# Value products of two head groups set beside the score products in TensorE's order, in an attention block on one core

## What is computed

```
x = _ln(src) * (1.0 + scale) + shift
q = (x @ Wq + bq).reshape(B, S, N_HEAD, HEAD_DIM).transpose(0, 2, 1, 3)
k = ...
v = ...
scores = jnp.einsum('bhqd,bhkd->bhqk', q / math.sqrt(HEAD_DIM), k)
scores = scores + attention_bias
scores = jnp.where(src_mask, -jnp.inf, scores.astype(jnp.float32))
probs = jax.nn.softmax(scores, axis=-1).astype(v.dtype)
ctx = jnp.einsum('bhqk,bhkd->bhqd', probs, v)
ctx = ctx.transpose(0, 2, 1, 3).reshape(B, S, D)
x = x + (ctx @ Wo + bo)
```

## Time and profile before

| | us |
|---|---|
| median of 3 runs | 1367.18 (1366.38 to 1367.87) |
| the profiled execution's own time | 1369.96 |
| its span, first to last instruction | 1367.8 |
| PE busy | 1321.2 (97%) |
| DVE busy | 1075.3 (79%) |
| ACT busy | 1071.8 (78%) |
| POOL busy | 871.5 (64%) |

### The profile page before, as it was taken

One profiled execution on the slowest core, in us unless ns is written; L12 is line 12 of the kernel. 1 busy time (PEld: TensorE's weight loads), 2 busy tenths in 40 slices (PEclk: granted clock), 3 DMA queues, 4 the chain that ended last, 5 costly groups with the idle time before them and its releaser, 6 DMA issues. The chain is left out here.

```text
span 1367.8 us, 39618 instructions
## 1 busy us (share of the span) xinstructions
PE 1321.2 (97%) x11936; PEld 1119.3 (82%) x11936; DVE 1075.3 (79%) x3638; ACT 1071.8 (78%) x2664; POOL 871.5 (64%) x874
## 2 busy tenths in 40 slices
PE   4999999999999999999999998789999999999997
PEld 3777777777777777777777776579999999999997
DVE  4777777787877777778778777578888888888885
ACT  1788888888888888888888886777777777777773
POOL 4999989989999998998999998311222222122210
PEclk9999999999999999999999999989999999999998
DMA  9546656555564665655556482101010110111100
GB/s 289 184 152 200 191 161 207 166 188 181 169 210 152 197 191 159 208 164 187 181 169 210 154 259 70 32 24 40 31 46 31 35 42 31 46 31 41 36 24 32
DMA packets 182670, 175.07 MB, mean 128 GB/s; under 512 B 15552, under 2 KB 182112, under 8 KB 182624
## 3 DMA queue, kind: packets, MB, share of 16 engines
q1 hardware_dynamic: 181248, 173.64, 40.1%
q10 hardware_dynamic: 1376, 0.85, 0.2%
HBM read 157.69 MB, written 16.78 MB: 128 GB/s over the span
## 5 line engine op out<-in xcount | busy, mean ns | idle before, releaser
L428 POOL TENSOR_TENSOR ring<-ring,maskv 128x1024 f32<-128x1024 f32 x256 | 600.0, 2373 | 12.4 <-DMA ring<-in_fside 5.1
L912 ACT ACTIVATE ring<-ring,nmax 128x256 f32<-128x256 f32 x1024 | 452.5, 501 | 24.6 <-DVE nmax L606 24.6
L606 DVE CUSTOM_DVE_ANT_0 ring<-bank,ring 128x256 f32<-128x256 f32 x1024 | 373.0, 418 | 90.4 <-PE bank L1176 73.5
L917 ACT ACTIVATE pT<-bank 128x512 f32<-128x512 f32 x416 | 239.5, 592 | 103.5 <-PE bank L1191 103.4
L1191 PE MATMUL bank<-ident,ring 128*128 128x128 f32 x2048 | 292.6, 278 | 1.4 <-ACT pT L917 1.1
L1191 PEld LDWEIGHTS bank<-ident,ring 128*128 128x128 f32 x2048 | 231.9, 143 | 70.6 <-issue 47.9
L1047 ACT ACTIVATE work<-bank,b1t 128x256 f32<-128x256 f32 x256 | 107.6, 476 | 109.0 <-PE bank L1390 109.0
L1176 PE MATMUL bank<-work 32*128 32x256 f32 x2048 | 148.4, 404 | 6.0 <-DVE nmax L606 5.2
L1390 PE MATMUL bank<-hT_high,w_high 128*128 128x256 f32 x512 | 147.9, 289 | 3.4 <-DVE hT_rest L781 3.4
L1403 PE MATMUL bank<-w_high,gT_high 128*128 128x256 f32 x512 | 148.1, 289 | 0.0
L1403 PE MATMUL bank<-w_rest,gT_high 128*128 128x256 f32 x512 | 145.3, 284 | 0.0
(11 more groups left out here) (162 smaller groups left out, 2730.5 us busy)
## 6 DMA issues: line engine op xcount, KB each, us to landing
ring<-in_fside SPq DMA_DIRECT2D x128, 1024.0 KB, 7.7
xt<-in_x SPq DMA_DIRECT2D x32, 256.0 KB, 3.2
x_d<-x2s SPq DMA_DIRECT2D x32, 256.0 KB, 7.8
work<-x_d SPq DMA_DIRECT2D x32, 256.0 KB, 2.8
out<-pT SPq DMA_DIRECT2D x32, 256.0 KB, 2.2
mk<-in_mask SPq DMA_DIRECT2D x32, 64.0 KB, 6.7
w<-in_W SPq DMA_DIRECT2D x2, 1024.0 KB, 10.5
wada<-in_W_ada SPq DMA_DIRECT2D x1, 512.0 KB, 8.1
```

Of the source, the lines that this page charges most:

```text
L428: nc.gpsimd.tensor_tensor(v, v, m, ALU.add).then_inc(s_masked, 1)
L606: nc.vector.tensor_tensor_reduce(out=v, in0=score_ps[h % HG][:, qt], in1=v, scale=-1.0, scalar=ROW_MAX_NEG, op0=ALU.add, op1=ALU.min, accu ...
L912: nc.scalar.activation(v, v, ACT.Exp, bias=nmax[:, b.par, h, qt:qt + 1], scale=-1.0).then_inc(s_exp, 1)
L917: nc.scalar.activation(pT[:, h % (2 * HG)], tp_ps[h % 2], ACT.Copy).then_inc(s_pta, 1)
```

## The change

Two of PE's four value products per batch move, and ACT's evictions of them. `pv(b-1, 3)` moves from behind `transposes(b, 3)` to behind `scores(b, 1)`; `pv(b, 0)` from behind the key projection to ahead of `scores(b, 3)`. On ACT, `pv_out(b-1, 2)` moves to the head of the body, `pv_out(b-1, 3)` to behind head 3's exponential, and `pv_out(b, 0)` to behind `gs_column`, ahead of head 8's copy. No instruction is added or left out, and DVE's, POOL's and SP's rows are the same. The numbers of all lines behind the first edit are one lower in the changed kernel.

```diff
@@ ACT's body @@
+                if tail:
+                    pv_out(b.plus(-1), 2)
                 if main:
                     exp_head(b, 1)
                     exp_head(b, 2)
                     copy_pT(b, 0)
                     exp_head(b, 3)
+                if tail:
+                    pv_out(b.plus(-1), 3)
+                if main:
                     copy_pT(b, 1)
                     copy_pT(b, 2)
                     exp_head(b, 4)
-                if tail:
-                    pv_out(b.plus(-1), 2)
-                if main:
                     exp_head(b, 5)
-                if tail:
-                    pv_out(b.plus(-1), 3)
-                if main:
                     exp_head(b, 6)
...
                     exp_head(b, 9)
-                    pv_out(b, 0)
                     exp_head(b, 10)
...
                     gs_column(b.n)
+                    pv_out(b, 0)
                     copy_pT(b, 8)
@@ PE's body @@
                     transposes(b, 0)
                     scores(b, 1)
+                if tail:
+                    pv(b.plus(-1), 3)
+                if main:
                     transposes(b, 1)
                     transposes(b, 2)
                 if prep:
                     project_qk(b.plus(1), 0)
                 if main:
                     transposes(b, 3)
-                if tail:
-                    pv(b.plus(-1), 3)
-                if main:
                     transposes(b, 4)
                     transposes(b, 5)
...
                 if prep:
                     project_qk(b.plus(1), 1)
                 if main:
-                    pv(b, 0)
                     transposes(b, 6)
                     transposes(b, 7)
                 if prep:
                     project_v(b.plus(1))
                 if main:
                     transposes(b, 8)
+                    pv(b, 0)
                     scores(b, 3)
```

## The result

The changed kernel takes 1384.29 us (median of 4 runs, 1383.33 to 1385.44), against 1366.99 before (4 runs, 1366.38 to 1367.87): ratio 1.0126, 95% interval 1.0109 to 1.0144. It is slower, as forecast, but by 17.3 us where 11.1 were forecast, and 1384.3 lies above the range's end of 1383. The profiled executions differ by 15.5 us of span (1383.3 against 1367.8). Of all timed runs in this document one, of 2177.74 us at a mean clock of 0.559 among the twelve of "group 0 alone", was in a slow state and is left out of its median.

What follows compares the result with a forecast made beforehand. PE, busy without waits in the attention stage, was taken as the bound. Per batch -0.30 + 0.57 + 0.17 = +0.44; 29 batches +12.8, batch 0 0.0, batch 30 -0.6, batch 31 -1.1: +11.1, 1378.3 us; range 1372 to 1383 (85%).

Steps and rivals of the forecast that it cites:

- What bounds the kernel: Attention stage: PE runs without waits, 26.29 us a batch, so its own instruction time counts and any wait adds in full.
- the saving: Two value products a batch placed beside scores: each saves 0.15 us of array switching, -0.30 a batch.
- Head 3's copy: Head 5's transposes wait 0.52 us for DVE to copy out head 3's result, plus 0.05 restart: +0.57 a batch.
- the first rival: Both waits on PE total under 0.30 us a batch, so the change is faster; with none, 1357.8 us; 5%.
- The key eviction: project_v waits 0.07 us for DVE's k_out to free their shared PSUM bank, plus 0.10 restart: +0.17 a batch.
- Batches 30 and 31: Last batches: PE's wait for DVE in 30 shrinks, -0.6 us; waits for ACT and context in 31 shrink, -1.1.
- the third rival: Behind batch 30's shorter wait the clock stays at its upper level, some 3 us come back: 1375 us; 13%.
- the saving alone: Value products beside scores: only the 0.15 us saved at each placement counts, no waits, 63 x 0.15 gives 1357.8; 5%.
- one term less: project_v's wait hidden (1373.1 us) or the scores-to-product switch free (1374.6): 12% for one; both, 1369.4: 3%.
- ACT being late: ACT's 0.8 us slip isn't covered; transposes wait for exponentials, 0.3 to 0.8 a batch: 1385 to 1400 us; 7%.

Runs made afterwards that it cites:

- group 0 alone: Kernel before with only group 0's product and its eviction on ACT moved: 1370.62 us, ratio 1.002; a second profile of the same kernel: 1372.12 us.
- exchanged waits: Changed kernel with DVE's two waits ahead of copy_pT swapped, alone or with PE's two ahead of transposes: 1386.14 us (one run) alone, 1380.02 us with both.
- `ctx_natural` in the gap: Changed kernel with the query projection split around head 3's transposes, plus ctx_natural(b-1, 1) behind the key projection and DVE's second-half normalisation behind k_out: 1360.72 us.

## Why the prediction was right in direction and too low

**What bounds the kernel** and **the saving** held: no idle time took up the new waits, each placement beside scores saves 0.15, and the direction that no row had shown (scores at 412.29, product at 413.37, transposes at 414.37) takes 1.08 and 1.00, as the shown one did. The Trainium skill's "TensorEngine Tiling (Array Packing)", Key Properties, names a drain for a change of mode. These rows agree with it: the direct change between the two tiled shapes was not cheaper than the way over the whole array.

**Head 3's copy** was right in its mechanism and mis-sized in its term. +0.57 was taken from batch 0 and is exactly what the unrolled batches show: 26.733 against the forecast 26.73. The loop's batches pay 0.16 more, 26 x 0.16 = 4.2 us. The failed step is the claim, made against the first rival, that the wait's parts "don't depend on the batch": batch 0 is unrolled, and its waits are for constants, while in the hardware loop a wait's value has to be worked out in registers, and the step that does it can stand between the wait that ends last and the instruction. The runs with exchanged waits took the 0.16 away in two halves, 0.09 on DVE and 0.07 on PE, and the traces' records list the register instructions that carried the deciding waits; what such an instruction costs by itself was not measured. With the 0.16 the forecast would have been 1382.5, near the upper end of its range.

**The key eviction** (+0.17) held in the run of group 0 alone: 26.313 is 0.026 more than before, 0.02 was forecast. The 0.05 from the copy's end to PE is 0.06 in its own row (42.26 to 42.32), within the 0.07 to 0.08 measured for the wait. With `ctx_natural` in the gap the wait was gone (26.167 to 26.037).

**Batches 30 and 31**: the wait before scores is 3.83 instead of 4.61 (3.6 forecast). The detour begins the expected 1.0 earlier, but its first instruction takes 1.77 instead of 1.55. As group 0 alone gained nothing here, with 2.52, this term held in part by luck. From batch 30's head 14 to batch 31's `gs_gram` (854.22 to 872.30 before, 871.25 to 888.20 now) it is -1.1, as forecast. The clock's spell was the third rival, and it half came, in the profiled execution: PE's timeline behind that wait, as in the earlier trace rows:

```profile
865.89 1.98 PE L1175 MATMUL bank<-work 32*128 32x256 f32 x16 [3.83 <-DVE nmax L606]
...
869.52 1.89 PE L1277 MATMUL bank<-wo,ctxT 128*128 128x256 f32 x8
```

and the same projection before:

```profile
851.18 3.20 PE L1278 MATMUL bank<-wo,ctxT 128*128 128x256 f32 x8
```

project_o at 869.52 runs at the upper level again, where before it had still been slow; 1.5 us come back. No run shows that the shorter wait did this, as the rival had it, and two speak against it. With only DVE's waits exchanged the wait is 3.77 and the granted clock from 863 to 871 us 0.57, so the spell is as long as before; with group 0 alone the wait is 4.58 and the spell came short once and long once. The 1.5 us are chance as far as the runs show.

**What no term had** is the start. With the same order and the same work, PE's key projection of batch 0 ran at the lower clock in the changed kernel's profile, first below, and at the upper one before, second:

```profile
26.04 3.78 PE L1233 MATMUL bank<-xT,wkp 128*128 128x256 f32 x8 [1.50 <-DVE work L625]
```

```profile
26.08 1.99 PE L1234 MATMUL bank<-xT,wkp 128*128 128x256 f32 x8 [1.50 <-DVE work L625]
```

3.78 against 1.99 busy, so 1.7 us by nothing that was changed, about what the other spell gave back. The sum of the profiles: +1.7 for the start, 30 x 0.446 + 26 x 0.16 = +17.5 to batch 30, -3.4 from there to batch 31 (0.8 wait, 1.5 clock, 1.1 batch 31), -0.4 behind it: +15.5, the spans' difference. The medians differ by 1.8 us more, as the profiled execution of before (1369.96) lay 3.0 above its median and that of the changed kernel (1385.44) 1.2. Spells would explain it, the two profiles of group 0 alone being 3.0 apart, but the timed runs left no traces. Against the later median of before, 1368.0, the change costs 16.3. Of the 6.2 us by which 17.3 exceeds the forecast 11.1, the loop's wait explains 4.2; the other 2.0 can't be put down to a term.

**The rivals**: the saving alone (whose 63 x 0.15 gives 1357.7, not 1357.8), one term less, and ACT being late fell. ACT being late looked right by the waits' view, which was the reason to test it: head 5's exponential had 0.8 us to spare.

## What to carry to other kernels

Before moving an item out from between two others, ask what needed the distance: here the product was the 1.0 us in which another engine emptied a buffer, and its removal cost 0.73 us a batch (0.57 + 0.16), where the move saved 0.15; splitting a neighbour and putting half of it there kept the saving. A bound taken from an unrolled iteration is not one for the hardware loop, where a wait that decides may have a register step behind it; of two waits on one instruction the deciding one was best coded last in the loop and first in unrolled code, which the period of either shows. A releaser's name is a guess by time: check whether the waiting instruction needs that very item, and compare periods of the loop rather than whole times where the spread outside it is larger than the effect.

## What was not expected of the hardware

- In the hardware loop, a wait that decides costs 0.09 us more on DVE and 0.07 us more on PE where another wait is coded behind it (26.893, 26.803 and 26.733 us a batch for none, one and both exchanged), while in unrolled code the same exchanges cost 0.07 each (26.733, 26.80, 26.866).
- A projection directly behind tiled products, or behind a wait of even 0.08 us, takes 0.10 us more (1.83 against 1.73), four transposes behind scores or a wait 0.05 (0.58 against 0.53).
- Spells at the lower clock of the same kernel, in the same place and behind the same wait of 4.58 us, last 3.4 or 6.9 us, and between the stages, worked out in the same way from 0.67 and 0.51 over 21 us, 13.9 or 20.6 us; the two executions differ by 3.0 us.
- A DVE instruction of the same shape in the same place (L677, 128x2048) took 1.55 us in the kernel before, 1.77 in the changed one and 2.52 with group 0 alone, which decides how much an earlier start in batch 30 gives; the cause was not tested.
